# Two layers of graph attention: four places for layer 1's attention blocks, output rows and input landings, and finished rows first in a step

## The reference

```python
# layer 0
q = x @ Wq + bq;  k = x @ Wk + bk;  v = x @ Wv + bv        # 8 heads of 64
scores = einsum('bqhd,bkhd->bhqk', q, k) / 8 + (1 - adj) * -1e9
x1 = layernorm(x + (softmax(scores) @ v) @ Wo + bo)
# layer 1: other weights, no output projection, mask where adj == 0
y  = layernorm(x1 + softmax(scores1(x1)) @ v1(x1))
```

## Time and profile before

| | |
|---|---|
| time, median of 3 runs | 3168.12 us (3167.33 to 3170.53) |
| time of the profiled execution | 3165.01 us |
| its span, first to last instruction | 3163.2 us |
| mean granted clock of TensorE | 0.970 |
| busy: TensorE matmuls, VectorE, ScalarE, GpSimd | 95%, 59%, 49%, 43% |
| mean busy share of the DMA engines, SyncE's queue | 46.5% |

### The profile page before, as it was taken

The page is one execution under the profiler, slowest core; times in us unless marked ns, Lnnn a source line. Parts: engine busy times, 40 slices in busy tenths (PEclk is TensorE's granted clock), DMA queues, the critical chain, the costliest instruction groups (busy, mean ns, idle before and its releaser), DMA issues.

```text
span 3163.2 us, 58261 instructions
## 1 busy us (share of the span) xinstructions
PE 2999.1 (95%) x18956; PEld 2536.4 (80%) x18956; DVE 1850.6 (59%) x7060; ACT 1557.8 (49%) x5135; POOL 1354.6 (43%) x1285
## 2 busy tenths in 40 slices
PE   7999999999999999999999999999899989999995
PEld 5888888888888888888888877777777777777774
DVE  4556565656565565656566565555556555555655
ACT  4535354544445353545454555455445545554553
POOL 3445555555555454554544333333333333333332
PEclk9999999999999999999999999999999999999997
DMA  5354434444444444344454544554454455455445
GB/s 181 93 142 113 134 107 134 118 123 131 115 137 113 140 115 134 107 134 117 124 149 132 158 119 138 147 138 126 142 155 117 137 147 139 125 144 153 117 137 147
DMA packets 411010, 417.71 MB, mean 132 GB/s; under 512 B 46113, under 2 KB 308513, under 8 KB 410657
## 3 DMA queue, kind: packets, MB, share of 16 engines
q1 hardware_dynamic: 409408, 413.32, 46.5%
q10 hardware_dynamic: 1296, 0.67, 0.1%
HBM read 145.37 MB, written 103.81 MB: 79 GB/s over the span
## 4 chain that ended last, share of the span: by engine, by line
PE 53%; SPq 14%; DVE 12%; DMA 10%; issue 6%; POOL 4%; ACT 1%; DVEq 0%; POOLq 0%; ACTq 0%
PE ring L320 23%; PE ring L328 22%; SPq L235 7%; DVE prob L579 6%; SPq L218 5%; PE ring L363 4%; DMA out<-x 4%; PE ring L352 4%; DMA x_raw<-x_feat 4%; POOL xt_lo L732 3%; DVE turned L597 2%; DMA at_lo<-x_bias 2%; POOL prob L742 1%; DVE x_res L627 1%; SPq L203 1%
## 5 line engine op out<-in xcount | busy, mean ns | idle before, releaser
L479 ACT ACTIVATE prob<-prob,neg_max 128x128 f32<-128x128 f32 x2048 | 791.7, 393 | 259.4 <-DVE neg_max L579 259.4
L742 POOL TENSOR_TENSOR prob<-prob,inv_sum 128x512 f32<-128x512 f32 x512 | 522.2, 1041 | 645.3 <-DVE inv_sum L587 645.3
L459 ACT ACTIVATE k_all<-ring,bk_col 128x512 f32<-128x512 f32 x256 | 311.2, 1216 | 661.7 <-PE ring L320 661.5
L732 POOL TENSOR_TENSOR xt_lo<-x_raw,xt_hi 128x512 fp32r<-128x512 f32 x254 | 331.9, 1316 | 607.6 <-DVE xt_hi L554 607.6
L554 DVE CAST xt_hi<-x_raw 128x512 fp32r<-128x512 f32 x254 | 196.5, 794 | 545.7 <-DMA x_raw<-x_feat 545.7
L579 DVE CUSTOM_DVE_ANT_0 prob<-ring,mask 128x128 f32<-128x128 f32 x2048 | 440.1, 283 | 116.5 <-PE ring L352 116.4
L466 ACT ACTIVATE q_all<-ring,bq_col 128x512 f32<-128x512 f32 x256 | 176.7, 690 | 486.2 <-PE ring L320 486.2
L328 PE MATMUL ring<-w_hi_v,xt_hi 128*128 128x512 f32 x1024 | 406.9, 397 | 8.3 <-DVE neg_max L579 8.3
L597 DVE STREAM_TRANSPOSE turned<-prob 128x512 f32<-128x512 f32 x512 | 347.4, 697 | 114.8 <-POOL prob L742 110.2
L320 PE MATMUL ring<-xt_hi,w_hi_k 128*128 128x512 f32 x1024 | 399.4, 390 | 13.6 <-DVE w_lo_k L542 13.6
L328 PE MATMUL ring<-w_hi_v,xt_lo 128*128 128x512 f32 x1024 | 399.4, 390 | 0.0
(11 more groups left out here) (63 smaller groups left out, 4786.3 us busy)
## 6 DMA issues: line engine op xcount, KB each, us to landing
prob_t<-turned SPq DMA_DIRECT2D x1024, 128.0 KB, 2.8
x_res<-x_tok SPq DMA_DIRECT2D x256, 256.0 KB, 3.6
x_raw<-x_feat SPq DMA_DIRECT2D x254, 256.0 KB, 3.4
x_feat<-x_turned SPq DMA_DIRECT2D x512, 64.0 KB, 2.1
x_tok<-x_bias SPq DMA_DIRECT2D x128, 256.0 KB, 2.3
at_lo<-x_bias SPq DMA_DIRECT2D x512, 64.0 KB, 2.1
out<-x SPq DMA_DIRECT2D x128, 256.0 KB, 3.7
prob<-w_k SPq DMA_DIRECT2D x2, 512.0 KB, 6.7
```

Of the source, the lines that this page charges most:

```text
L459: act.activation(k_all[:, m, :].rearrange("p (b j n) -> p b n j", b=QB, n=SQ), ring[K_BANK[m]][:].rearrange("p (b n j) -> p b n j", b=QB, ...
L479: last = act.activation(prob[b][:, i, n, :], prob[b][:, i, n, :], ACT.Exp, bias=neg_max[b][:, i, n:n + 1], scale=-1.0, accum_out=row_sum[b ...
L732: pool.tensor_tensor(features(xt_lo[s % 2], b), raw_view(raw), features(xt_hi[s % 2], b).bitcast(F32), ALU.subtract).then_inc(x_lo_set, 1)
L742: pool.tensor_tensor(prob[b][:, i], prob[b][:, i], inv_sum[b][:, i, :].unsqueeze(2).to_broadcast([P, NC, NODES]), ALU.mult).then_inc(norm_ ...
```

## The change

Layer 1 gets four places of each kind, made of tiles that only layer 0 used as pairs. x1_bias and x1_turned together are blocks1[0] to blocks1[3]: the turned attention of graph b goes there, is carried from there, and later the same tile takes the graph's output rows. x1[0] and x1[1] are free then and serve as landings of inputs 2 and 3. ScalarE's attention_out is removed: VectorE's transposes read ring[b] in PSUM. TensorE's waits for the removed copy become waits for the transposes. The orders of VectorE, GpSimd and SyncE's queue change in both layers, as the diff shows. (Lines with "..." are left out; the rest of the diff is declarations of semaphores, and the final wait for the stores.)

```diff
+        def raw_of(quad, b):
+            return x1[b - 2] if quad >= G + 3 and b >= 2 else x_raw[b % 2]
+        blocks1 = x1_bias + x1_turned
...
             def load_raw(s, b, layer):
...
-                sp.wait_ge(x_lo_set, QB * s + b - 1)
-                sp.dma_start(x_raw[b % 2][:], src).then_inc(raw_in[b], 16)
+                if s <= G + 2 or s == G + 3 and b < 2:
+                    sp.wait_ge(x_lo_set, QB * s + b - 1)
+                elif s == G + 3:
+                    sp.wait_ge(x1_turned_set, N0)
+                    sp.wait_ge(x1_bias_set, N0)
+                else:
+                    sp.wait_ge(x_lo_set, QB * s + b - 3)
+                sp.dma_start(raw_of(s, b)[:], src).then_inc(raw_in[b], 16)
             def carry_attention(a, b):
...
-                                 x1_bias[b % 2][n * SQ:(n + 1) * SQ].rearrange("p (n k) -> p n k", n=BLK)
+                                 blocks1[b][n * SQ:(n + 1) * SQ].rearrange("p (n k) -> p n k", n=BLK)
             def store_y(a, b):
                 sp.wait_ge(ln_set, QB * a + b + 1)
-                sp.dma_start(out[a - G, b], x1[b % 2][:]).then_inc(y_out[b % 2], 16)
+                sp.dma_start(out[a - G, b], blocks1[b][:]).then_inc(y_out[b], 16)
             def step(s):                                   # SyncE's queue
+                early = 4 if s + 1 >= G + 3 else 2
                 if nxt is not None:
-                    load_raw(s + 1, 0, nxt)
-                    load_raw(s + 1, 1, nxt)
+                    for b in range(early):
+                        load_raw(s + 1, b, nxt)
...
                 if nxt is not None:
-                    load_raw(s + 1, 2, nxt)
-                    load_raw(s + 1, 3, nxt)
+                    for b in range(early, QB):
+                        load_raw(s + 1, b, nxt)
...
-                if s <= LAST:
-                    turn_probs(s, 0)
                 if la == 1:
                     carry_attention(a, 0)
                     carry_attention(a, 1)
                 if s <= LAST:
-                    turn_probs(s, 1)
+                    turn_probs(s, 0)
                 if la == 1:
                     carry_attention(a, 2)
                     carry_attention(a, 3)
+                if s <= LAST:
+                    turn_probs(s, 1)
...
@@ tensor: both waits for the copy
-                            pe.wait_ge(scaled_set, QB * (s - 2 - G) + m + 1)
+                            pe.wait_ge(at1_blocks_set, QB * (s - 2 - G) + m + 1)
...
@@ scalar
-            def attention_out(a, b):
...
@@ vector
             def turn_attention(a, b):
...
+                dve.wait_ge(att_done, QB * a + b + 1)
+                if a > G:
+                    dve.wait_ge(y_out[b], 16 * (a - G))
+                elif b < 2:
+                    dve.wait_ge(x1_tok_out[b], 16 * 2 * G)
                 else:
-                    dve.wait_ge(x1_tok_out[b], 16 * 2 * G)
-                dve.transpose(x1_bias[b % 2][:].rearrange("p (n c f) -> p c n f", n=BLK, c=NC), attention_blocks(b)
-                              ).then_inc(at1_blocks_set, 1)
+                    dve.wait_ge(x1_feat_out[b - 2], 64 * 2 * G)
+                dve.transpose(blocks1[b][:].rearrange("p (n c f) -> p c n f", n=BLK, c=NC),
+                              ring[b][:].rearrange("p (c q n) -> p c n q", c=NC, n=BLK)).then_inc(at1_blocks_set, 1)
             def normalise(a, b):
...
+                if a < G:
                     need(dve, x1_turned_set, done - 2)
                     need(dve, x1_bias_set, done - 2)
...
+                    rows = x1[b % 2]
                 else:
-                    dve.wait_ge(y_out[b % 2], 16 * (2 * (a - G) + b // 2))
+                    dve.wait_ge(at1_in[b], 64 * (a - G + 1))
+                    rows = blocks1[b]
             def step(s):                                   # VectorE
-                if la is not None:
-                    turn_blocks(a, 2)
                 if lf is not None:
                     finish_start(f, 0)
+                    finish_start(f, 1)
                 if la is not None:
                     invert_sums(a, 3)
-                if lf is not None:
-                    finish_start(f, 1)
-                if la is not None:
-                    turn_blocks(a, 3)
+                    turn_blocks(a, 2)
                 if lf is not None:
                     finish_end(f, 0)
                     finish_end(f, 1)
                     finish_start(f, 2)
                     finish_start(f, 3)
+                if la is not None:
+                    turn_blocks(a, 3)
+                if lf is not None:
                     finish_end(f, 2)
                     finish_end(f, 3)
...
                     mask_scores(s, 3, lp)
-                    turn_blocks(s, 0)
+                    invert_sums(s, 1)
                 for b in range(QB):
                     if la == 0:
                         attention_low(a, b)
                     elif la == 1:
                         turn_attention(a, b)
                     if lp is not None and b == 1:
-                        invert_sums(s, 1)
+                        turn_blocks(s, 0)
...
             def step(s):                                   # GpSimd
-                if la is not None:
-                    normalise_probs(a, 2)
                 if lf is not None:
                     inverse_deviation(f, 0)
+                    inverse_deviation(f, 1)
                 if la is not None:
                     normalise_probs(a, 3)
...
                     normalise_probs(s, 0)
                     normalise_probs(s, 1)
+                    normalise_probs(s, 2)
```

More of the change, by code:

```diff
@@ L129, in adj_resnorm_kernel @@
         wo_done = sem("wo_done")
-        scaled_set = sem("scaled_set")
         at1_blocks_set = sem("at1_blocks_set")
@@ L142, in adj_resnorm_kernel @@
         x1_tok_out = [sem(f"x1_tok_out{i}") for i in range(2)]
-        y_out = [sem(f"y_out{i}") for i in range(2)]
+        y_out = [sem(f"y_out{b}") for b in range(QB)]
         LAST = 2 * G - 1
@@ L308, in _ @@
                 step(s)
-            for i in range(2):
-                sp.wait_ge(y_out[i], 16 * 2 * G)
+            for b in range(QB):
+                sp.wait_ge(y_out[b], 16 * G)
         @block.tensor
@@ L414, in step @@
                         else:
-                            pe.wait_ge(scaled_set, QB * (a - 1 - G) + b + 1)
+                            pe.wait_ge(at1_blocks_set, QB * (a - 1 - G) + b + 1)
                         attend(a, b)
@@ L518, in step @@
                         attention_high(a, b)
-                    elif la == 1:
-                        attention_out(a, b)
                 if lp is not None:
@@ L611, in turn_attention @@
             def turn_attention(a, b):
[L612 to L617, removed]
-                else:
-                    dve.wait_ge(x1_tok_out[b], 16 * 2 * G)
-                dve.transpose(x1_bias[b % 2][:].rearrange("p (n c f) -> p c n f", n=BLK, c=NC), attention_blocks(b)
-                              ).then_inc(at1_blocks_set, 1)
+                dve.wait_ge(att_done, QB * a + b + 1)
[3 more added lines that the diff above has]
+                    dve.wait_ge(x1_tok_out[b], 16 * 2 * G)
+                else:
+                    dve.wait_ge(x1_feat_out[b - 2], 64 * 2 * G)
+                dve.transpose(blocks1[b][:].rearrange("p (n c f) -> p c n f", n=BLK, c=NC),
+                              ring[b][:].rearrange("p (c q n) -> p c n q", c=NC, n=BLK)).then_inc(at1_blocks_set, 1)
             def residual1(a, b):
@@ L636, in statistics, with normalise @@
                 dve.tensor_scalar(var_eps[b], mean_var[b][:, 1:2], EPS, None, ALU.add).then_inc(eps_set, 1)
-            def normalise(a, b, layer):
+            def normalise(a, b):
                 done = QB * a + b + 1
                 dve.wait_ge(rstd_set, done)
-                if layer == 0:
+                if a < G:
                     need(dve, x1_turned_set, done - 2)
                     need(dve, x1_bias_set, done - 2)
-                elif isinstance(a, int) and a == G and b < 2:
-                    dve.wait_ge(x1_turned_set, N0)
-                    dve.wait_ge(x1_bias_set, N0)
-                else:
-                    dve.wait_ge(y_out[b % 2], 16 * (2 * (a - G) + b // 2))
-                dve.tensor_scalar(x1[b % 2][:], x_res[b][:], mean_var[b][:, 0:1], rstd[b],
+                    rows = x1[b % 2]
+                else:
+                    dve.wait_ge(at1_in[b], 64 * (a - G + 1))
+                    rows = blocks1[b]
+                dve.tensor_scalar(rows[:], x_res[b][:], mean_var[b][:, 0:1], rstd[b],
                                   ALU.subtract, ALU.mult).then_inc(ln_set, 1)
@@ L664, in finish_end @@
             def finish_end(f, b):
-                normalise(f, b, layer_of(f))
+                normalise(f, b)
                 if layer_of(f) == 0:
@@ L693, in step @@
                     for b in range(QB):
-                        x_high(s + 1, b, x_raw[b % 2])
```

(19 more changed lines are left out.)

2 lines of the change are left out of this document (removed).

## The result

The changed kernel takes 2996.34 us (median of 4 runs, 2995.82 to 2998.56), against 3169.01 us for the kernel before: a ratio of 0.9457, 95% interval 0.944 to 0.9473. The forecast was 2997.

The account below looks back on a forecast made before the run. TensorE bounds the kernel, but layer 1 loses time to late masking and lower clock. Savings 165.4 + 5.2 = 170.6 us; 3165.0 - 170.6 = 2994.4, plus 3.1 to the median, gives 2997 us; range 2985 to 3010.

Parts of the forecast that it names:

- TensorE's need, 40.29 us, and minus 165.4 us: Layer 1: without waits TensorE takes 40.29 us a step, not 46.00, at clock 1.00; 29 steps save 165.4 us.
- The walk through one step: Layer 1: one step laid out from S, its scores' start on TensorE; last casts S+31.5, next masking wanted S+41.6.
- the two new waits: Layer 1, VectorE: transposes of graphs 2 and 3 wait until turned probabilities of graphs 0 and 1 leave, S+19.5 and S+27.
- 10 us spare: Layer 1: 10 us between the last cast and the next masking, covering dearer PSUM transposes (2.8 us) or a late load.
- the 3.2 us of the earlier trace: Layer 1: four input loads, issued together, were each to land in 3.2 us, the last near S+30.
- The rival in which part of the wait remains: Layer 1: DMA contention uses up the 10 us, TensorE waits 1 to 2 us a step; 3026 to 3055 us; 9%.
- 3.55 us of wait and 2.15 of clock: Layer 1: loss per step split into TensorE's wait for masking (102.9 us in all) and lower clock (62.5 us).
- the clock stays down: Layer 1: TensorE sometimes runs at the lower clock though waits are gone; only 108 us won, 3060 us; 3%.
- The cover that I added on top: Layer 0: masking could end 1.65 us later; with VectorE's 2.45 us wait, 4.1 us cover a 1.3 us delay, price 0.
- The 2.6 us that step 32 loses stay: Seam of the layers: step 32 still takes 53.81 instead of 51.17 us, as landings there still share two places.
- the new order: Reordered VectorE, GpSimd and SyncE's queue: fits within layer 1's 40.29 us step; layer 0 masking 1.3 us later, price 0.
- Foretold 5.2 us: After the last scores: the queue reaches the carries at S+33.6 instead of S+38.9, minus 5.2 us; bounds 0 and 8.

## Why the prediction was right, and where not

**TensorE's need, 40.29 us, and minus 165.4 us.** Right to 0.1 us. One undisturbed step of the kernel before had shown it. The clock is 1.00 in all 29 steps, so the rival in which it stays down is out. The Trainium skill (TensorE: Matmul & The Clock Gate, HAM oscillation) has a gap in TensorE's work throttle the clock, so that the next work starts cold; these rows agree, as without gaps the granted clock is 1.00, where it was 0.94 with them.

**The walk through one step.** S+19.5, S+27 and S+31.5 for the two new waits and the last cast were S+19.3, S+27.2 and S+32.9. The "10 us spare" were 8.1 on average. The term that was too small is the landing: the 3.2 us of the earlier trace rows were taken for all four loads, and the second pair took a median 4.6. The new waits appeared where they were expected. The rival in which part of the wait remains needed the cover to be used up, and the run with 7.4 us of added work shows that even this much doesn't.

**Why the third load was late.** The prediction says that it may start only when GpSimd has read the first input from the same place. The semaphore is there, but the queue waited for it 0.9 us at the longest, 28.1 us in 43 waits between 1769 and 2900 us. For the rest the load stood behind other DMAs that the queue was still issuing. Four landings removed both, since all four loads are issued early, which is why the mistake did not cost the forecast anything.

**How close the total came.** The sum was 2997.5 us before rounding, the result 2996.34. Part of this is luck. The seam lost 3.1 us that the sum did not have, the end gained 1.3 more than it had, and the 3.1 us that were added because the profiled execution before was that far below its median were 0.1 this time. These misses nearly cancel.

**How the loss was split.** The prediction took 3.55 us of wait and 2.15 of clock as two prices a step that add up. Their sum was right, being read from the total. As prices they are not: the run with twenty transposes shows that the step is the loop's length and the clock no extra. So the size of the rival "the clock stays down", 3060 us, had no ground either: it took the 62.5 us of clock as a loss beside the waits, while by that run they lay inside the loop. I should have followed the loop from masking to masking, which is what the kernel before was bound by.

**What the parts are worth.** I listed row places and landings as two waits that go, and the order as something that brings new waits. Measured one at a time on the kernel before (the first two with the turn from PSUM): row places 0, landings 104 us, order 97 us. The forecast needed only that the loop fall under 40.29 us, which hides this.

**Layer 0.** Its steps stayed at 51.17 us. VectorE's wait for the scores, 2.45 us at the shortest before, is now:

```profile
909.65 0.29 DVE L578 CUSTOM_DVE_ANT_0 prob<-ring,mask 128x128 f32<-128x128 f32 x1 [0.91 <-PE ring L362]
```

0.91 us at the shortest. It was to fall by about 1.3 us and fell by 1.5. The cover that I added on top, 1.65 us from the attends, was not needed and isn't shown. TensorE has no wait in the thirty steps, as foretold.

**The seam.** "The 2.6 us that step 32 loses stay" failed: 5.8 us are lost. What failed is taking the price of "the new order" as 0 there too: graph 2's turned probabilities stand in front of the first finished row in the queue, behind the splits of the weights, and this step had no cover left. With the old order and all else of the change that row is issued 17.7 us ahead of the scores, as in the kernel before, and the step is 54.11 us: by this one trace the order makes 2.8 of the 3.1 us. Over all traces except those with the splits moved, this step took 53.8 to 56.0 us with the old order (waits of 2.6 to 3.1 us) and 56.7 to 59.2 with the new one (3.6 to 5.0). In the changed kernel the queue came to that row 1.1 us later (1659.16, before 1658.07), the third cast 1.5 us later (1680.77, before 1679.23), and TensorE's wait grew by the same 1.45 us (4.02, before 2.57). The attends ran at the low clock, the first sixteen in 1.78 us where it had been 1.09, and all of them together took 1.7 us longer. In this single step that is paid in full, since 1.45 + 1.7 is the 3.1 us that the step grew. The run that moves the splits gives it back.

**The end.** Foretold 5.2 us, measured 6.5. The carries start at 2976.42, S+35.0, where 33.6 was said, but are issued in 10.6 us instead of 12.3, and what follows them is 1.0 us shorter. So of the 5.2 us only 3.8 came from where they were foretold.

## What to carry to other kernels

Measure the loop: from one pass of the late work to the same work of the next pass. If it is longer than the bound engine's own work, a step costs the loop, and a wait beside its path is worth nothing however long it is (97 us of waits for stores, gone, gained nothing); where several parts each shorten the loop, the last ones to be added seem worthless and the first too large. What is taken out below the bound is cover, and one can find how much by adding work until the time moves.

## What the runs showed of the hardware

Four 256 KB loads issued together within 2 us left a small mark on their neighbours: stores behind them landed in a median 4.0 to 4.2 us, and the second pair of loads in 4.6, the first in 3.1 us. In the run with the changed kernel and two landings, stores landed in 3.8 to 3.9 us. A block transpose of 128x512 out of PSUM with a strided read took 0.68 to 0.69 us on average, as out of SBUF (0.69 in the kernel before).
